# Mask rows inside the exponents' product of a fused attention and mixture-of-experts kernel

## The reference

```python
fg_mat = cs[..., :, None] - cs[..., None, :]          # cs: cumulated log-sigmoid of the forget gates
log_D = jnp.where(mask, fg_mat + igate[..., None, :], -jnp.inf)   # mask: lower triangle
D = jnp.exp(log_D - max_log_D)
C = (q @ k.T / sqrt(DH)) * D
C_norm = C / (maximum(abs(sum(C)), exp(-max_log_D)) + EPS)
h = C_norm @ v                                         # then a layernorm per head, times a weight
x = x + h
```

## Time and profile before

| | |
|---|---|
| runs | 697.56, 697.69, 697.80 us (median 697.69) |
| profiled execution | 699.08 us, its span 697.0 us |
| TensorE matmul | 599.0 us busy, 86% of the span |
| VectorE | 479.0 us, 69% |
| ACT | 315.7 us, 45% |
| GpSimd | 306.7 us, 44% |
| granted TensorE clock | 0.936 of full speed on average |
| chain that ended last | TensorE 71%, VectorE 15%, DMA 5%, issue 3%, ACT 2% |

### The profile page before, as it was taken

How to read it: one execution, slowest core, us unless ns; L and a number is a source line. 1 busy time by engine, 2 the same in 40 slices (tenths; PEclk the granted TensorE clock), 3 DMA queues, 4 the chain that set the end, 5 groups by cost and what they waited for, 6 DMA issues and landing times.

```text
span 697.0 us, 14852 instructions
## 1 busy us (share of the span) xinstructions
PE 599.0 (86%) x3480; PEld 465.8 (67%) x3481; DVE 479.0 (69%) x1039; ACT 315.7 (45%) x704; POOL 306.7 (44%) x312
## 2 busy tenths in 40 slices
PE   3874499999999997411799999999999999999993
PEld 1331266676667665311588888888888888888883
DVE  3663447778787887899367676767677676767673
ACT  2454344545445453100455555555555555555551
POOL 2223435463645545000355454555555454555532
PEclk9998599999999999555799999999999999999997
DMA  8995545556564653351132433333332333333332
GB/s 272 294 305 170 176 134 158 177 171 180 164 196 156 174 166 105 104 205 8 39 63 47 62 49 58 53 54 53 54 61 46 62 49 58 53 54 56 51 46 24
DMA packets 71673, 76.77 MB, mean 110 GB/s; under 512 B 12830, under 2 KB 63780, under 8 KB 71652
## 3 DMA queue, kind: packets, MB, share of 16 engines
q1 hardware_dynamic: 55652, 50.27, 23.0%
q0 software_dynamic: 15712, 25.73, 20.3%
q10 hardware_dynamic: 288, 0.52, 0.2%
HBM read 53.29 MB, written 23.21 MB: 110 GB/s over the span
## 4 chain that ended last, share of the span: by engine, by line
PE 71%; DVE 15%; DMA 5%; issue 3%; ACT 2%; SPq 1%; POOL 1%; DVEq 0%; ACTq 0%; POOLq 0%
PE bank L1270 10%; PE bank L1272 10%; PE bank L1271 9%; PE bank L1168 6%; PE bank L1184 6%; PE bank L1302 5%; PE bank L1298 5%; PE bank L1299 5%; PE bank L1285 4%; DMA qT_scratch<-qt 3%; PE bank L1257 2%; PE bank L1233 2%; PE bank L1165 2%; PE bank L1163 2%; DVE ohn L934 2%
## 5 line engine op out<-in xcount | busy, mean ns | idle before, releaser
L1090 POOL DMA_INDIRECT out_rows<-ys,index x71 | 113.5, 1599 | 153.7 <-DVE ys L986 145.2
L1270 PE MATMUL bank<-w12l,xh 128*128 x284 | 120.3, 424 | 2.2 <-DVE xl L958 2.2
L1272 PE MATMUL bank<-w12h,xh 128*128 x284 | 112.4, 396 | 0.0
L1271 PE MATMUL bank<-w12h,xl 128*128 x284 | 112.2, 395 | 0.0
L992 DVE TENSOR_TENSOR w3l<-w,w3h 128x1024 fp32r<-128x1024 f32 x71 | 87.2, 1228 | 31.0 <-issue 30.0
L1081 POOL DMA_INDIRECT xg<-token_table,index x71 | 70.5, 993 | 74.9 <-DVE index L951 53.0
L1184 PEld LDWEIGHTS bank<-aug,c 128*128 128x128 f32 x512 | 67.1, 191 | 29.9 <-issue 24.4
L656 ACT CAST w3h<-w 128x1024 fp32r x71 | 74.4, 1048 | 20.0 <-issue 20.0
L1298 PE MATMUL bank<-w3l,hth 128*128 128x256 f32 x284 | 76.5, 302 | 1.8 <-DVE w3l L992 1.8
L641 ACT ACTIVATE sg<-bank 128x512 f32<-128x512 f32 x71 | 42.6, 599 | 76.2 <-PE bank L1272 76.2
L782 DVE SCALAR_TENSOR_TENSOR c<-bank,d 128x512 f32<-128x512 f32 x64 | 44.1, 690 | 46.3 <-PE bank L1184 38.0
(11 more groups left out here) (164 smaller groups left out, 1087.0 us busy)
## 6 DMA issues: line engine op xcount, KB each, us to landing
x<-in_x SPq DMA_DIRECT2D x32, 256.0 KB, 3.3
wst<-in_w12T POOLq DMA_DIRECT2D x26, 256.0 KB, 3.6
aug<-in_ctxv SPq DMA_DIRECT2D x16, 264.0 KB, 3.0
ct<-in_ctxT SPq DMA_DIRECT2D x16, 256.0 KB, 4.5
qT_scratch<-qt SPq DMA_DIRECT2D x16, 256.0 KB, 3.7
kt<-in_ctxT SPq DMA_DIRECT2D x16, 256.0 KB
qbd<-qT_scratch SPq DMA_DIRECT2D x64, 64.0 KB
out_rows<-x SPq DMA_DIRECT2D x16, 256.0 KB, 2.2
```

What stands on the lines that cost most here:

```text
L1090: q.indirect_dma_start(out=out, out_offset=bass.IndirectOffsetOnAxis(ap=index[:, j:j + 1], axis=0), in_=YS[o][:], in_offset=None, compute_ ...
L1270: mm(acc, XH[i][:, k, :], wl, start=(k == 0), stop=False)
L1271: mm(acc, XL[i][:, k, :], wh, start=False, stop=False)
L1272: ins = mm(acc, XH[i][:, k, :], wh, start=False, stop=(k == NK - 1))
```

## The change

The exponents' block loses its mask matmul. `LG` and `RM` grow from 27 to 92 rows: row r of the 64 new ones holds in `RM` -1e30 for the queries that lie before r in their half of 64, and in `LG` a one at key r (first half) or key r + 64 (second half); the last row masks the keys from 64 on for the first half of the queries. So `LG` exists twice, once for each half of the queries, and the block becomes two matmuls of 256 columns (4 heads x 64 queries) instead of two of 512. The 24 rows of the keys' term are therefore loaded twice per step, from `g_scratch`, into the two halves of `LG`.

The constants of these rows are no longer among the late constants but are issued by SP behind the loads of the gates and ahead of `load_scores(0, 0)`; TensorE waits for them with a semaphore of their own. ACT copies `X2T` and takes `weights(3)` before it squares. On VectorE the small constant is added to the columns once, in the transition, and `wmax` and `wden` become one operation.

```diff
 MASKED = -1e30
+HALF = P // 2
+GROWS = PARTS * (NH + 1)
+MROWS = GROWS + HALF + 1
@@
         onwb = sb("onwb", [P, NH, DH], on=early)
-        mask4 = sb("mask4", [P, HG * P], BF16, on=early)
         wst = [sb(f"wst{i}", [P, HID], on=early) for i in range(2)]
         KVB = [sb(f"kvb{i}", [P, NG, HG, DV], on=early) for i in range(2)]
-        RM = [sb(f"rm{i}", [PARTS * (NH + 1), NH, S], BF16, on=early) for i in range(2)]
-        LG = [sb(f"lg{i}", [PARTS * (NH + 1), S], BF16, on=early) for i in range(2)]
+        RM = [sb(f"rm{i}", [MROWS, NH, S], BF16, on=early) for i in range(2)]
+        LG = [sb(f"lg{i}", [MROWS, 2, S], BF16, on=early) for i in range(2)]
         QBD = [sb(f"qbd{i}", [P, NG, HG, S], on=early) for i in range(2)]
@@
         X2T = sb("x2t", [P, NC * NK, P], on=m)
-        wabs, wmax, wden, rec, mu, var, z, z2, lnz, zp, sc = (
+        wabs, wden, rec, mu, var, z, z2, lnz, zp, sc = (
             sb(n, [P, NC * NH], on=m)
-            for n in ("wabs", "wmax", "wden", "rec", "mu", "var", "z_", "z2_", "lnz", "zp", "sc"))
+            for n in ("wabs", "wden", "rec", "mu", "var", "z_", "z2_", "lnz", "zp", "sc"))
         st3 = sb("st3", [P, NC, 6], on=m)
@@
         hots_ready, inverted, tables, codes_in = sems("hots_ready", "inverted", "tables", "codes_in")
-        clear_ready, may_add, slot_consts = sems("clear_ready", "may_add", "slot_consts")
+        clear_ready, may_add, slot_consts, mask_rows = sems("clear_ready", "may_add", "slot_consts", "mask_rows")
         y_added = two("y_added")
@@
-                for dst, src in ((ib, ibias), (fb, fbias), (id_b, identb), (mask4, maskT), (io, iota)):
+                for dst, src in ((ib, ibias), (fb, fbias), (io, iota)):
                     sp.dma_start(dst[:], src).then_inc(late_consts, 16)
...
                 sp.dma_start(onwb[:], onw.rearrange("p (h d) -> p h d", h=NH)).then_inc(late_consts, 16)
-                for i in range(2):
-                    sp.dma_start(LG[i][0:PARTS, :], marks[0:PARTS, 0:S]).then_inc(late_consts, 16)
-                    sp.dma_start(RM[i][PARTS:PARTS * (NH + 1), :, :],
-                                 marks[PARTS:PARTS * (NH + 1), :].rearrange("q (h s) -> q h s", h=NH)
-                                 ).then_inc(late_consts, 16)
@@
+            for i in range(2):
+                for lo, hi in ((0, PARTS), (GROWS, MROWS)):
+                    sp.dma_start(LG[i][lo:hi, :, :], lgc[lo:hi, :].rearrange("q (a s) -> q a s", a=2)
+                                 ).then_inc(mask_rows, 16)
+                sp.dma_start(RM[i][PARTS:, :, :], rmc[PARTS:, :].rearrange("q (h s) -> q h s", h=NH)
+                             ).then_inc(mask_rows, 16)
+
             def load_scores(b, i):
@@
                     wait(sp, s_ready, 2 * NG * (b - 1))
-                    sp.dma_start(LG[i][PARTS:, :], g_dram[b].rearrange("q h s -> (q h) s")).then_inc(in3[i], 16)
+                    for a_ in range(2):
+                        sp.dma_start(LG[i][PARTS:GROWS, a_, :], g_dram[b].rearrange("q h s -> (q h) s")
+                                     ).then_inc(in3[i], 16)
                     sp.dma_start(RM[i][0:PARTS, :, :],
@@
                 weights(2)
+                if has(b, 3):
+
+                    act.wait_ge(x2t_psum, b - 2)
+                    wait(act, score_psum, b - 3)
+                    nc.scalar.copy(X2T[:].rearrange("p k s -> p (k s)"), bank[7][:]).then_inc(x2t_ready, 1)
+                weights(3)
                 if has(b, 1):
@@
                                          TOT[o][:, :, 0:DH], ACT.Square).then_inc(sq_ready, 1)
-                if has(b, 3):
-
-                    act.wait_ge(x2t_psum, b - 2)
-                    wait(act, score_psum, b - 3)
-                    nc.scalar.copy(X2T[:].rearrange("p k s -> p (k s)"), bank[7][:]).then_inc(x2t_ready, 1)
-                weights(3)
                 if has(b, 2):
@@
             dve.wait_ge(cols_psum, 1)
-            v.tensor_copy(cols[:].rearrange("p a q -> p (a q)"), bank[0][:]).then_inc(cols_ready, 1)
+            v.tensor_copy(cols[:, 0:2].rearrange("p a q -> p (a q)"), bank[0][:, 0:2 * P])
+            v.tensor_scalar(cols[:, 2:4].rearrange("p a q -> p (a q)"), bank[0][:, 2 * P:], NORM_EPS, None,
+                            ALU.add).then_inc(cols_ready, 1)
@@
-            K3 = 7
+            K3 = 6
@@
                     st.then(v.scalar_tensor_tensor(wabs[:], sums, -1.0, sums, ALU.mult, ALU.max))
-                    st.then(v.tensor_tensor(wmax[:].rearrange("p (c h) -> p c h", c=NC),
-                                            wabs[:].rearrange("p (c h) -> p c h", c=NC),
-                                            cols[:, 2:4, bass.ds(pb * NH, NH)], ALU.max))
-                    st.then(v.tensor_scalar(wden[:], wmax[:], NORM_EPS, None, ALU.add))
+                    st.then(v.scalar_tensor_tensor(wden[:].rearrange("p (c h) -> p c h", c=NC),
+                                                   wabs[:].rearrange("p (c h) -> p c h", c=NC), NORM_EPS,
+                                                   cols[:, 2:4, bass.ds(pb * NH, NH)], ALU.add, ALU.max))
                     v.reciprocal(rec[:], wden[:])
@@
             pe.wait_ge(late_consts, 16 * N_LATE)
+            pe.wait_ge(mask_rows, 16 * N_ROWS)
@@
                     wait(pe, d_ready, k - 1)
-                    mm(bank[n % 2][:], LG[i][:, c * P:(c + 1) * P],
-                       RM[i][:, hg * HG:(hg + 1) * HG, c * P:(c + 1) * P], start=True, stop=False)
-                    mm(bank[n % 2][:], id_b[:], mask4[:], start=False, stop=True).then_inc(e_ready, 1)
+                    for a_ in range(2):
+                        at = c * P + a_ * HALF
+                        ins = mm(bank[n % 2][:].rearrange("p (h q) -> p h q", h=HG)[:, :, a_ * HALF:(a_ + 1) * HALF],
+                                 LG[i][:, a_, c * P:(c + 1) * P],
+                                 RM[i][:, hg * HG:(hg + 1) * HG, at:at + HALF], start=True, stop=True)
+                    ins.then_inc(e_ready, 1)
@@
     token = p + P * np.arange(NT)[None, :]
-    marks = np.ones((PARTS * (NH + 1), NH * S), np.float32)
-    marks[PARTS:] = np.tile(np.repeat(np.eye(NH), S, axis=1), (PARTS, 1))
+    key, row = np.arange(S) % P, np.arange(HALF)[:, None]
+    lgc = np.ones((MROWS, 2, S), np.float32)
+    lgc[GROWS:MROWS - 1] = np.stack([key[None] == row, key[None] == row + HALF], axis=1)
+    lgc[MROWS - 1] = np.stack([key >= HALF, np.zeros(S)])
+    rmc = np.full((MROWS, NH, S), MASKED, np.float32)
+    rmc[PARTS:GROWS] = np.tile(np.eye(NH)[:, :, None], (PARTS, 1, S))
+    rmc[GROWS:MROWS - 1] = np.where(row > np.arange(S) % HALF, MASKED, 0.0)[:, None]
     ins = {
@@
         "ident": np.eye(P, dtype=np.float32),
-        "identb": np.eye(P).astype(bf),
-
-        "maskT": np.tile(np.where(p > q, MASKED, 0.0), (1, HG)).astype(bf),
+        "lgc": lgc.reshape(MROWS, -1).astype(bf),
+        "rmc": rmc.reshape(MROWS, -1).astype(bf),
         "trib": np.concatenate([p < q, np.ones((P, P))], axis=1).astype(bf),
-        "marks": marks.astype(bf),
         "iota": np.broadcast_to(q, (P, P)).astype(np.float32),
```

More of the change, by code:

```diff
@@ L77, in then, with build @@
         self.eng.wait_ge(self.sem, self.base + self.n)
-def build(nc, x, ctx, ctxv, ctxT, gkq, gkk, gkv, ibias, fbias, onw, w12T, w3T, gateT, ident, identb,
-          maskT, trib, marks, iota, iota16, codes, floors, spares, out):
+def build(nc, x, ctx, ctxv, ctxT, gkq, gkk, gkv, ibias, fbias, onw, w12T, w3T, gateT, ident, lgc, rmc, trib, iota, iota16, codes, floors, spares, out):
     qT_dram = nc.dram_tensor("qT_scratch", (B, P, NG, S), F32).ap()
@@ L108, in build @@
         id_f = sb("id_f", [P, P])
-        id_b = sb("id_b", [P, P], BF16)
         tri = sb("tri", [P, 2, P], BF16)
@@ L312, in flat @@
             return t[:].rearrange("p k s -> p (k s)")
-        N_CONST, N_LATE = 4, 12
+        N_CONST, N_LATE, N_ROWS = 4, 6, 6
         PIECES0, PIECES2 = (0, 2), tuple(range(4, B, 2))
@@ L325, in build @@
         K1 = 2 * NC
-        LOADS3 = 1 + HG + 2
+        LOADS3 = 1 + HG + 3
         LOADSV = 3
```

## The result

The changed kernel took 710.76 us (median of 4 runs, 709.16 to 714.43), the kernel before 697.75 us beside it: ratio 1.0192, 95% interval 1.0147 to 1.0237. It is 13 us slower, where 683.4 us had been predicted. The profiled execution took 714.43 us, its span is 712.4 us, 15.4 more than before.

The account below looks back on a forecast made before the run. TensorE was taken as the narrow bound, with SP's two-step loop showing after the change. Gains of 4.0, 9.4, 0.6 and 0.8 less 0.5 us gave 14.3: 684.8 profiled, 683.4 median, range 671 to 691.

Parts of the forecast that it names:

- Part 5: First stage and transition: moving the constants saves 0.8 us in the first stage and costs 0.4, at most 2.4, behind gating loads.
- Part 1: Exponents' block on TensorE: 0.65 us falls to 0.22 to 0.32, saving 1.6 us a step, from 11.72 to about 10.1.
- Part 4: SP's queue: a second `LG` load adds 0.56 us per step to a two-step loop, making steps 11.4 us.
- the eleven steps: Attention from first exponents of step 4 to those of step 15: 12.25 us a step falls to 11.4, gaining 9.4 us.
- the loop: From `x2n` through SP's loads, `vw`, GpSimd's run and VectorE's centring to `x2n` two steps later: 23.25 us, reducible to 22.7.
- Part 2: ACT's copy of `X2T` before the square: removes the scores' stall, within 0.53 us a step; nothing taken beyond the step length.
- Part 3: One VectorE operation fewer (`wmax`): worth nothing or 2 us, taken as nothing; copying columns in two pieces costs 0.1 us once.
- the ends: Around the eleven steps: first four gain about 4.0 us, last step and tail 0.6, first stage 0.8, transition -0.5.
- Rival 3: SP's loop already sets the step, so the second `LG` load adds 4.2 us: slower, 702 us; chance 0.04.
- Rival 1: TensorE stays the bound, the loop falls apart, steps of 10.1 to 10.5 us: 670 us (667 to 676); chance 0.23.
- Rival 2: The exponents save little, weight loads staying exposed at 0.52 us a block: 688 us (686 to 692); chance 0.17.
- Rival 4: No change: gain and added issues cancel, 697.7 us; chance 0.02.

Follow-up runs that it names:

- e1: The changed kernel with the constant rows padded with zeros so their loads move 96 and 72 partitions instead of 89 and 65: 685.25 us, ratio 0.9809.
- e7: The padded 96-row kernel with SP's store and residual load later, GpSimd's weight load and `w12l` ahead of `vw`, one `LG` load per step: 668.97 us, ratio 0.9563.
- e11: The kernel before, mask still a matmul, with ACT's copy first, SP's store and residual load later, GpSimd's weight load and `w12l` ahead of `vw`: 691.59 us.
- e8: The kernel before with `LG` and `RM` zero-filled from 27 to 99 contracted rows, mask still its own matmul: 699.05 us, ratio 0.9999.
- e5: The padded 96-row kernel with SP's store behind the next step's `LG`, `RM`, `KT`, `QBD` loads and the residual's load behind `QTB`: 672.92 us, ratio 0.9605.
- e3: The padded 96-row kernel with one load of `LG` per step for both halves instead of two: 685.18 us, ratio 0.9813.
- e4: The padded 96-row kernel with ACT's old order (square, then copy and fourth exponential) put back: 690.08 us, ratio 0.986.
- e10: The kernel before with one edit, ACT's copy of `X2T` and fourth exponential ahead of the square: 694.21 us, ratio 0.9939.

## Why the prediction was wrong

**Part 5: constants moved** is the step that failed. It priced 0.7 MB behind the gating loads at 300 GB/s, the rate of the first stage, and put the transition at +0.4, at most +2.4 us. The two large loads ran at 26 GB/s, and the first exponents came 27.6 us late, 26.2 of them behind the gates' loads. The step had looked at bytes, issues and place, and not at how a load is shared out: the loads of the earlier trace rows that moved at 300 GB/s have other shapes, and the step took their rate for one of 89 rows. No row of the kernel before shows such a load; what would have asked the question is that the diff makes a load of 89 rows out of one of 24. The rule of the Trainium skill cited above answers it, and the prediction didn't use it. Nearly all of the miss lies here: with 96 rows (e1), first exponents come at 80.26 and the time is 685.25 us. Beside this a slip in the sum is small: the six issues move 0.87 MB, not 0.7, since `LG`'s 65 rows add 0.13 MB, which at the step's own rate is 0.5 us more.

**Part 1: the exponents.** Right. Block 0.22 at the lower bound, no 0.1 going in; TensorE's step 10.05 to 10.17 in e7, forecast 10.1; saving 1.6 a step (e11 against e7). That the 27 rows made the gaps was argued from the earlier trace rows, and e8 shows it by itself.

**Part 4: SP's queue, and the eleven steps.** 11.4 us were forecast and 11.40 measured, and the waits stand where the loop said: TensorE idle for `QBD`, `vw` for `QTB`, the centring held until `w12l` ends. `x2n` ended at 208.54 and 231.48, 22.9 us apart, forecast 22.7. e5 cut the loop at SP and the step fell to 10.41. The 0.56 us for the second `LG` was too much: e3 gave back 0.12 a step. So the loop is shown; that its length came out to the hundredth is in part luck, since this term was too high and 11.4 had been rounded up from 11.3.

**Part 2: copy before square.** Mis-sized. It was taken at nothing beyond the step length; it is worth 4.8 us (e4, e10). This hangs together with a reading that was partly wrong, "TensorE is the bound, though not by much": e8 took 0.8 us a step off TensorE's work and its eleven steps got 0.07 us shorter, e10 took nothing off and gained 4.8. The stall of 0.90 in the earlier trace rows was the end of a loop (`w12l`, centring, square, copy, scores), and the forecast saw its links and not that it sets the step beside TensorE. The sum came out all the same, since the change does both things at once.

**Part 3 and the ends.** The first four steps gave 3.7 us (forecast 4.0): the first three gained 1.6 or 1.7 each, the fourth lost 1.3 (13.42 us instead of 12.16). The eleven gave 9.4 (9.4), last step and tail 0.2 (0.6). The VectorE operation wasn't tried alone. First stage and transition together were forecast as 0.3 us gained, and e1 measures 0.3 lost: its gates' loads are issued 0.7 us earlier than before (63.73), and from there to the first exponents it takes 1.0 longer. But in the nine traces whose first stage is that of the changed kernel these loads come at 63.3 to 65.8 us, so the 0.8 of the first stage is neither borne out nor refuted.

**The rivals.** Rival 3, the only one that was slower, named SP's loop and the transition, but with 2.4 us at most there, and 702 us. The measured time lies beyond it and its mechanism didn't occur, since the steps got shorter. Its case was also argued by a misreading: `tot`'s 11 waits for `sc` come on top of `vw`'s 14 for `QTB`, not instead of them. Rivals 1 and 2 didn't occur: e7 reaches rival 1's time, but only with other queues. Rival 4, no change, didn't occur either.

## What to carry to other kernels

When an edit changes the number of rows of a large load, ask how that number divides: here 89, 94, 88 and 96 rows began the next stage 27.6, 14.5, 1.4 and 0.3 us late, and seven rows of zeros in each load were the whole cure. A stretch in which the DMA share is a sixteenth or an eighth, with SP's issues taking microseconds instead of 0.4, is the sign of it. And a step at 97% of one engine may still be held by a loop across the others: try the orders of the queues together with the smaller work, for here the mask rows were worth 9.0 us without the one and 22.6 with it.

## What was not expected of the hardware

- A load of 89 rows moved 26 GB/s at a DMA share of 0.06, one of 94 rows 53 GB/s at 0.13 (while other transfers were few), and the loads around e1's 96 rows 244 to 312 GB/s.
- An issue on SP behind two such loads took 12.43 us instead of 0.53 before and 0.40 in e1.
- A VectorE operation with two SBUF inputs waited longer than one GpSimd operation lasts. The centring began at 225.02, while GpSimd was issuing its weight load (224.70 to 225.26), and was held through the `w12l` behind it: 2.10 us, 1.41 over its own 0.69, where `w12l` takes 1.28. The prediction had said that by the rule of the Trainium skill (SBUF — State Buffer, Who interferes with whom) alone a wait could never exceed 1.28. All three of the longest in the eleven steps began during such an issue. The issue doesn't hold every such operation: this one, of VectorE, began ahead of the issue, during a product, and ended 0.05 us after it.

```profile
270.36 0.93 DVE L827 SCALAR_TENSOR_TENSOR tot<-mu,tot 128x512 f32<-128x512 f32 x1
```

```profile
269.42 1.33 POOL L1072 TENSOR_TENSOR x<-x,tot 128x256 f32<-128x256 f32 x2
270.68 0.56 POOL L1020 DMA_DIRECT2D wst<-in_w12T  x1
```

So this operation, which had waited since before the issue, ended beside it, and the three that began during an issue were held until the `w12l` behind it had ended. Why is not shown, and the profile's times of GpSimd are rough.
